# A 1024-step tanh recurrence on one core: split early sum, full tanh in PSUM, sums seeded by copies, rolled loops

## The chip, the cores and the metric

The kernel runs on one core of one Trainium2 chip. The metric is the device time of one execution in microseconds (us), lower is better. The kernel before was timed in three runs.

## The reference

The input `x` is 2 sequences of 1024 steps with 256 channels. Two residual layers follow each other. The first is a per-sequence 256x256 matrix (a base matrix plus a low-rank part made from a conditioning vector); the second is a recurrence over the 1024 steps:

```python
x = x + _L0_cond_ref(x, cond, ...)      # x + x @ layer, so y = 2 x + x @ layer
xW = einsum('ntd,dh->nth', y, Wx) + b
def step(prev_h, xw):
    next_h = tanh(prev_h @ Wh + xw)     # h0 = cond
x = y + h_t                             # every step's state is added to the output
```

Each step depends on the one before, and a step's work is tiny: two vectors of 256 channels. Channels lie on partitions, so a state is a tile of 128 partitions by 4 columns: 2 channel halves `m` times 2 sequences `b` (`COLS` = 4).

## The kernel before, in words

**Exact products from f16.** Weights are split into a high and a low f16 part (`wh_s[:, 0]`, `wh_s[:, 1]`), scaled by 256. The state of step u is used in three f16 forms: `h_pre`, an early estimate; `h_rnd`, the rounded full state; `h_lo`, the difference between the full f32 state `h_f` and `h_pre`.

**One step of the chain** (`chain_step`, L312 on PE; L467 to L476 on ACT; L560 on DVE). PE keeps two sums for the next state. The early sum lies in the PSUM bank `pre` and needs only `h_rnd` times the high weights (4 matmuls); ACT turns it into `h_pre` of the next step. The full sum lies in the bank `acc` and needs `h_pre` times high and low weights (8 matmuls) and `h_lo` times the high weights (4 matmuls); ACT turns it into `h_f` (L462) and `h_rnd` (L464). DVE makes `h_lo` from `h_f` and `h_pre` (L563). The order of PE's 16 matmuls is written out by hand, with a wait ahead of each new operand:

```python
pe.wait_ge(s_hpre[half], u + 1)      # 7 matmuls with h_pre follow
pe.wait_ge(s_hrnd[half], u + 1)      # 4 with h_rnd, the last signals s_presum; 1 with h_pre
pe.wait_ge(s_hlo[half], u + 1)       # 4 with h_lo, the last signals s_sum
```

**Side work.** The 1024 steps are 32 blocks of 32, each of two halves A and B of 16 steps. Between the steps PE also does the block's other matmuls: `layer_products` (L275, 32 a block, first layer of the next block), `input_products` (L283, the products with `Wx` and the bias). The latter are done three times a half, into `pre` and into the two banks `acc` for even and odd steps: 54 matmuls a half. `turn_x` and `turn_out` (L265, L270) are f32 transposes; `turn_out` in step 1 of a half is followed by three semaphore clears (`clear_states`, L306). DVE does the splits, the sum with y (`sum_out`) and the copy of the output rows (`row_out`) between its `h_lo`.

**Code.** PE, ACT and DVE run fully unrolled code: 21105 matmuls, each with a weight load. Only SyncE, which issues the loads of `x_in` and the stores of `o_row`, has a loop over blocks (L230).

## Time and profile before

| | before |
|---|---|
| median of 3 runs | 792.67 us (791.72 to 792.92) |
| the profiled execution | 791.64 us |
| its span, first to last instruction | 789.8 us |
| matmuls, and busy share of PE | 21105, 93% |
| busy share of ACT and DVE | 50%, 33% |
| granted clock of TensorE | 1.00 throughout |

The busy share of PE is a union of overlapping matmuls: one lasts about 165 ns in the records, though PE starts the next one long before. To see how fast PE could go one has to look at the distance between starts, not at the busy share.

### The profile page before, as it was taken

The page shows a single profiled execution, that of the slowest core. Times are in us where ns is not written, and L with a number is a line of the kernel's source. Part 1 is how long each engine was busy: PE and PEld are TensorE (multiplying, and loading weights), DVE is VectorE, ACT ScalarE, POOL GpSimd, SP SyncE. Part 2 cuts the span into 40 slices and gives each one's busy share as a digit, 9 for nine tenths or more (in the row PEclk, how much of TensorE's full clock was granted, in tenths as well). Part 3 has the DMA queues.
Part 4 walks back from the last instruction along what each step waited for, and adds up shares of the span by engine and source line. Part 5 has one row for each costly group of instructions (what it writes and reads, how often), then busy time and mean ns, then how long its engine had stood idle before and what let it go on. Part 6 is the DMA issues. An engine that isn't in the chain of part 4 may idle for free.

```text
span 789.8 us, 48134 instructions
## 1 busy us (share of the span) xinstructions
PE 736.8 (93%) x21105; PEld 679.7 (86%) x21105; DVE 258.3 (33%) x1411; ACT 396.4 (50%) x3092; POOL 6.4 (1%) x18
## 2 busy tenths in 40 slices
PE   6699999999999999999999999999999999999996
PEld 5688888888888888888888888888888888888885
DVE  6433333333333333332333332323333333333322
ACT  6355545555555555555555554555555555554554
POOL 3000000000000000000000000000000000000000
DMA  7000000000000000000000000000000000000000
GB/s 271 7 10 9 11 11 9 7 11 9 10 11 9 7 11 9 10 10 10 7 10 10 10 10 10 10 8 10 10 10 10 10 7 9 11 10 9 8 7 6
DMA packets 12285, 12.51 MB, mean 16 GB/s; under 512 B 1813, under 2 KB 11056, under 8 KB 12080
## 3 DMA queue, kind: packets, MB, share of 16 engines
q1 hardware_dynamic: 11984, 9.45, 4.1%
q8 instruction: 166, 2.72, 1.4%
q14 instruction: 39, 0.32, 0.1%
q0 software_dynamic: 96, 0.02, 0.0%
HBM read 7.36 MB, written 2.10 MB: 12 GB/s over the span
## 4 chain that ended last, share of the span: by engine, by line
PE 88%; ACT 6%; issue 3%; DMA 1%; SPq 1%; DVE 1%; DVEq 0%; another core or an unknown queue 0%
PE acc L320 48%; PE pre L320 16%; PE p_y L278 8%; PE acc L297 7%; ACT h_pre L456 6%; PE pre L297 4%; PE p_xo L273 2%; PE p_xo L268 1%; DMA x_in<-x_dram 1%; PE acc L294 1%; PE pre L294 1%; SPq L212 1%; PE p_y L413 0%; SPq L209 0%; DVE lay_s L684 0%
## 5 line engine op out<-in xcount | busy, mean ns | idle before, releaser
L320 PE MATMUL acc<-h_pre,wh_s 128*128 128x2 f16 x8192 | 504.8, 168 | 35.7
L320 PEld LDWEIGHTS acc<-h_pre,wh_s 128*128 128x128 f16 x8192 | 378.5, 106 | 90.6 <-ACT h_pre L456 73.5
L456 ACT ACTIVATE h_pre<-pre 128x4 f16<-128x4 f32 x1023 | 178.0, 174 | 377.8 <-PE pre L320 377.8
L563 DVE TENSOR_TENSOR h_lo<-h_f,h_pre 128x4 f16<-128x4 f32 x1024 | 166.8, 163 | 512.6 <-ACT h_f L462 511.5
L320 PE MATMUL pre<-h_rnd,wh_s 128*128 128x2 f16 x4092 | 263.4, 168 | 0.0
L320 PE MATMUL acc<-h_lo,wh_s 128*128 128x2 f16 x4096 | 250.9, 165 | 0.0
L320 PEld LDWEIGHTS pre<-h_rnd,wh_s 128*128 128x128 f16 x4092 | 190.6, 108 | 0.0
L320 PEld LDWEIGHTS acc<-h_lo,wh_s 128*128 128x128 f16 x4096 | 188.4, 104 | 0.0
L462 ACT ACTIVATE h_f<-acc 128x4 f32<-128x4 f32 x1024 | 177.9, 174 | 0.6 <-PE acc L320 0.6
L464 ACT ACTIVATE h_rnd<-acc 128x4 f16<-128x4 f32 x1022 | 173.2, 169 | 0.0
L297 PE MATMUL acc<-y_s,wx_s 128*128 128x16 f16 x2048 | 101.8, 175 | 0.0
L278 PE MATMUL p_y<-x_s,lay_s 128*128 128x32 f16 x1024 | 89.8, 236 | 2.2 <-DVE lay_s L684 2.2
L297 PEld LDWEIGHTS acc<-y_s,wx_s 128*128 128x128 f16 x2048 | 79.3, 104 | 0.1
L278 PEld LDWEIGHTS p_y<-x_s,lay_s 128*128 128x128 f16 x1024 | 59.9, 120 | 2.7 <-DVE lay_s L684 2.7
L297 PE MATMUL pre<-y_s,wx_s 128*128 128x32 f16 x1024 | 58.1, 188 | 0.0
L297 PEld LDWEIGHTS pre<-y_s,wx_s 128*128 128x128 f16 x1024 | 42.1, 104 | 0.0
L294 PE MATMUL acc<-ones,b_w 128*128 128x16 f16 x256 | 25.8, 174 | 1.4 <-DVE y_s L543 1.4
L273 PE MATMUL p_xo<-ident,o_sum 128*64 128x128 f32 x64 | 25.7, 402 | 0.6 <-DVE o_sum L552 0.6
L558 DVE COPY o_row<-p_xo 64x128 f32<-64x128 f32 x64 | 18.1, 283 | 4.6 <-remote 1.6
L294 PEld LDWEIGHTS acc<-ones,b_w 128*128 128x128 f16 x256 | 16.8, 104 | 1.5 <-issue 1.5
L268 PE MATMUL p_xo<-ident,x_in 128*128 128x128 f32 x32 | 14.6, 455 | 0.7 <-DMA x_in<-x_dram 0.7
L552 DVE TENSOR_TENSOR o_sum<-y_cur,h_f 128x64 f32<-128x64 f32 x64 | 14.0, 219 | 0.6 <-ACT h_f L462 0.6
(77 smaller groups left out, 161.1 us busy)
## 6 DMA issues: line engine op xcount, KB each, us to landing
w_f<-w_dram SPq DMA_DIRECT2D x8, 512.0 KB, 7.6
x_in<-x_dram SPq DMA_DIRECT2D x32, 64.0 KB, 2.3
out_dram<-o_row SPq DMA_DIRECT2D x64, 32.0 KB, 1.9
w_f<-w_dram SPq DMA_DIRECT2D x1, 256.0 KB, 2.7
base_f<-base_dram SPq DMA_DIRECT2D x1, 256.0 KB, 10.2
wh_f<-wh_dram SPq DMA_DIRECT2D x1, 256.0 KB, 9.8
wx_f<-wx_dram SPq DMA_DIRECT2D x1, 256.0 KB, 9.9
cond_r<-cond_dram SPq DMA_DIRECT2D x1, 2.0 KB
```

Of the source, the lines that this page charges most:

```text
L268: nc.tensor.transpose(p_xo[:, 0:P], x_in[:, :], ident[:, :]).then_inc(s_xturn, 1)
L273: nc.tensor.transpose(p_xo[0:HALF * COLS, 0:P], o_sum[:, :], ident[:, :]).then_inc(s_oturn, 1)
L278: last = nc.tensor.matmul(py[:, :, mo, bb], lay_s[:, pw, bb, ki, mo * P:(mo + 1) * P], x_s[:, px, :, ki, bb], start=(bb, mo, ki, pw, px) = ...
L294: nc.tensor.matmul(dst, b_w[:, out_channels], ones[:, 0:n * NB], start=mo == 0, stop=True, skip_group_check=True)
L297: nc.tensor.matmul(dst, wx_s[:, pw, ki, out_channels], y_s[:, py, t, ki, :], start=False, stop=True, skip_group_check=True)
L320: return nc.tensor.matmul(dst[:, mo, :], wh_s[:, pw, ki, mo * P:(mo + 1) * P], h[:, par, ki, :], start=False, stop=True, skip_group_check= ...
L456: nc.scalar.activation(h_pre[:, n % 2].rearrange("p m b -> p (m b)"), src, func, scale=scale).then_inc(s_hpre[(n // HALF) % 2], 1)
L462: nc.scalar.activation(h_f[:, (n - 1) % BLOCK, :], src, func, scale=scale).then_inc(s_hf[half], 1)
L464: nc.scalar.activation(h_rnd[:, n % 2].rearrange("p m b -> p (m b)"), src, func, scale=scale).then_inc(s_hrnd[half], 1)
L552: nc.vector.tensor_add(o_sum[:, :], cols(y_cur[:, steps]), h_f[:, steps, :].rearrange("p t c -> p (t c)")).then_inc(s_osum, 1)
L558: nc.vector.tensor_copy(o_row[:, :], p_xo[0:HALF * COLS, 0:P]).then_inc(s_orow, 1)
L563: nc.vector.tensor_sub(h_lo[:, par].rearrange("p m b -> p (m b)"), h_f[:, slot, :], h_pre[:, par].rearrange("p m b -> p (m b)")).then_inc( ...
```

## The change

- **Two-piece early part.** `pre` becomes two banks, one for each channel half `m`. PE signals `s_presum` after each 2 of the 4 `h_rnd` matmuls, and ACT makes `h_pre` in two activations of 2 columns, each with its own signal. PE waits for them one by one: 4 matmuls with channel half 0 of `h_pre`, 4 with half 1. All 8 now stand ahead of the `h_rnd` matmuls (7 before).
- **f32 tanh to PSUM.** The full state that DVE needs is written to a PSUM bank `p_f`; DVE subtracts from there. A third activation of the full sum writes `h_f` in SBUF for the output (`s_hkeep`).
- **Seeded sums.** `input_products` writes only `pre` (18 matmuls a half). DVE copies the even and odd steps from there into the two `acc` banks, now shared by both halves (`seed`); PE takes `s_seed` ahead of steps 10 and 11 of a half.
- **Side work moved.** Input products in steps 2 to 4 of a half, all 32 layer products in steps 8 to 12 of half A, `turn_x` in step 5, the semaphore clears in steps 6 and 7. `x_s` and the layer's sum are laid out with the step innermost.
- **Loops.** PE, ACT and DVE run the 30 middle blocks in a hardware loop each (`Fori`), whose body is one block of 32 steps.

```diff
-        acc = [[pb(f"acc{half}{par}", [P, 512]) for par in range(2)] for half in range(2)]
-        pre = [pb(f"pre{half}", [P, 512]) for half in range(2)]
-        p_xo = pb("p_xo", [P, 512])
-        p_y = pb("p_y", [P, 512])
+        acc = [pb(f"acc{par}", [P, 512]) for par in range(2)]
+        pre = [pb(f"pre{half}", [P, NM, 512]) for half in range(2)]
+        p_w = pb("p_w", [P, 512])
+        p_f = pb("p_f", [P, 512])
...
-        PRE = 2
-        INPUT = [(slot, *product) for slot in (0, PRE, 1) for product in PRODUCTS]
-        BEFORE = 2 * len(PRODUCTS)
+        INPUT = sorted(PRODUCTS, key=lambda product: product[0])
...
+        FILL, LAYERS, SEED = 2, 8, 10
+        def z_cols(half, u):
+            at = (half * (HALF // 2) + u // 2) * COLS
+            return slice(at, at + COLS)
...
             def input_products(half, todo):
...
+                t = slice(half * HALF, (half + 1) * HALF)
+                for mo, ki, pw, py in todo:
+                    dst = pre[half][:, mo, 0:HALF * NB]
...
             def chain_step(half, u, last=False):
                 par = u % 2
-                full = acc[half][par][:, (u // 2) * COLS:(u // 2 + 1) * COLS].rearrange("p (m b) -> p m b", b=NB)
-                early = pre[half][:, u * COLS:(u + 1) * COLS].rearrange("p (m b) -> p m b", b=NB)
+                full = acc[par][:, z_cols(half, u)].rearrange("p (m b) -> p m b", b=NB)
                 def onto(dst, pw, mo, ki, h):
-                    return nc.tensor.matmul(dst[:, mo, :], wh_s[:, pw, ki, mo * P:(mo + 1) * P], h[:, par, ki, :],
+                    return nc.tensor.matmul(dst, wh_s[:, pw, ki, mo * P:(mo + 1) * P], h[:, par, ki, :],
                                             start=False, stop=True, skip_group_check=True)
-                pe.wait_ge(s_hpre[half], u + 1)
-                for mo, ki in TILES:
-                    onto(full, 1, mo, ki, h_pre)
-                for mo, ki in TILES[:3]:
-                    onto(full, 0, mo, ki, h_pre)
+                for ki in range(NM):
+                    pe.wait_ge(s_hpre[half], NM * u + ki + 1)
+                    for mo in range(NM):
+                        for pw in range(2):
+                            onto(full[:, mo, :], pw, mo, ki, h_pre)
                 if not last:
                     pe.wait_ge(s_hrnd[half], u + 1)
-                    for mo, ki in TILES:
-                        done = onto(early, 0, mo, ki, h_rnd)
-                    done.then_inc(s_presum[half], 1)
-                for mo, ki in TILES[3:]:
-                    onto(full, 0, mo, ki, h_pre)
+                    for mo in range(NM):
+                        for ki in range(NM):
+                            done = onto(pre[half][:, mo, u * NB:(u + 1) * NB], 0, mo, ki, h_rnd)
+                        done.then_inc(s_presum[half], 1)
                 pe.wait_ge(s_hlo[half], u + 1)
                 for mo, ki in TILES:
-                    done = onto(full, 0, mo, ki, h_lo)
+                    done = onto(full[:, mo, :], 0, mo, ki, h_lo)
                 done.then_inc(s_sum[half], 1)
-            def half_a(first=False, last=False):
+            def half_steps(half, first=False, last=False):
                 for u in range(HALF):
-                    chain_step(A, u)
-                    if first and u == 0:
-                        input_products(A, INPUT[BEFORE:])
-                    if not first and u == 1:
+                    if u >= SEED and u < SEED + 2 and not (last and half == B):
+                        take(pe, s_seed[u % 2], 1)
+                    chain_step(half, u, last=last and half == B and u == HALF - 1)
+                    if u == 1 and not first:
                         turn_out()
-                        clear_states(B)
-                    if 2 <= u < 10:
-                        input_products(B, share(INPUT, 7, u - 2))
-                    if last:
-                        continue
-                    if u == 10:
-                        turn_x()
-                    if u == 13:
-                        take(pe, s_xsplit, 1)
-                    if 13 <= u < HALF - 1:
-                        layer_products(share(EARLY, 4, u - 13))
-            def half_b(last=False):
-                for u in range(HALF):
-                    chain_step(B, u, last=last and u == HALF - 1)
-                    if u == 1:
-                        turn_out()
-                        clear_states(A)
-                    if last:
-                        continue
-                    if u == 0:
-                        layer_products(share(LATE, 5, 0))
-                    if 2 <= u < 6:
-                        product = layer_products(share(LATE, 5, u - 1))
-                    if u == 5:
-                        product.then_inc(s_ymm, 1)
-                    if u == 9:
-                        take(pe, s_ysplit, 1)
-                    if 9 <= u < HALF - 1:
-                        input_products(A, share(INPUT, 9, u - 9))
+                    if FILL <= u < FILL + 3 and not (last and half == B):
+                        if u == FILL and half == B:
+                            take(pe, s_ysplit, 1)
+                        filled = input_products(1 - half, share(INPUT, 6, u - FILL))
+                        if u == FILL + 2:
+                            filled.then_inc(s_fill, 1)
+                    if u == 6 and not first:
+                        clear_states(1 - half)
+                    if u == 7 and not first:
+                        pe.sem_clear(s_hlo[1 - half])
+                    if half == A and not last:
+                        if u == 5:
+                            turn_x()
+                        if u == LAYERS:
+                            take(pe, s_xsplit, 1)
+                        if LAYERS <= u < LAYERS + 5:
+                            product = layer_products(share(LAYER, 7, u - LAYERS))
+                        if u == LAYERS + 4:
+                            product.then_inc(s_ymm, 1)
...
-            input_products(A, INPUT[:BEFORE])
-            half_a(first=True)
-            for _ in range(NBLOCK - 2):
-                half_b()
-                half_a()
-            half_b()
-            half_a(last=True)
-            half_b(last=True)
+            input_products(A, INPUT).then_inc(s_fill, 1)
+            for par in range(2):
+                take(pe, s_seed[par], 1)
+            half_steps(A, first=True)
+            with pe.Fori(0, NBLOCK - 2):
+                half_steps(B)
+                half_steps(A)
+            half_steps(B)
+            half_steps(A, last=True)
+            half_steps(B, last=True)
             turn_out()
...
         def _(act):
-            def give_pre(n, src, func, scale):
-                nc.scalar.activation(h_pre[:, n % 2].rearrange("p m b -> p (m b)"), src, func,
-                                     scale=scale).then_inc(s_hpre[(n // HALF) % 2], 1)
-            def give_h(n, src, func, scale, rounded=True):
+            def give_pre(n, m, src, func, scale):
+                nc.scalar.activation(h_pre[:, n % 2, m, :], src, func, scale=scale).then_inc(s_hpre[(n // HALF) % 2], 1)
+            def give_h(n, src, func, scale, rounded=True, final=False):
                 half = (n // HALF) % 2
-                nc.scalar.activation(h_f[:, (n - 1) % BLOCK, :], src, func, scale=scale).then_inc(s_hf[half], 1)
+                if not final:
+                    nc.scalar.activation(p_f[:, 0:COLS], src, func, scale=scale).then_inc(s_hf[half], 1)
                 if rounded:
                     nc.scalar.activation(h_rnd[:, n % 2].rearrange("p m b -> p (m b)"), src, func,
                                          scale=scale).then_inc(s_hrnd[half], 1)
+                nc.scalar.activation(h_f[:, (n - 1) % BLOCK, :], src, func, scale=scale).then_inc(s_hkeep[half], 1)
             def half_block(half, first=False, last=False):
                 for u in range(HALF):
                     final = last and u == HALF - 1
                     n = half * HALF + u + 1
                     if not final:
-                        act.wait_ge(s_presum[half], u + 1)
-                        give_pre(n, pre[half][:, u * COLS:(u + 1) * COLS], ACT.Tanh, 1.0 / SCALE)
+                        for m in range(NM):
+                            act.wait_ge(s_presum[half], NM * u + m + 1)
+                            give_pre(n, m, pre[half][:, m, u * NB:(u + 1) * NB], ACT.Tanh, 1.0 / SCALE)
                     act.wait_ge(s_sum[half], u + 1)
-                    give_h(n, acc[half][u % 2][:, (u // 2) * COLS:(u // 2 + 1) * COLS], ACT.Tanh, 1.0 / SCALE,
-                           rounded=not (last and u >= HALF - 2))
+                    give_h(n, acc[u % 2][:, z_cols(half, u)], ACT.Tanh, 1.0 / SCALE,
+                           rounded=not (last and u >= HALF - 2), final=final)
...
             half_block(A, first=True)
-            for _ in range(NBLOCK - 2):
+            with act.Fori(0, NBLOCK - 2):
                 half_block(B)
...
+            def seed(half, par):
+                early = pre[half][:, :, 0:HALF * NB].rearrange("p m (t q b) -> p t q m b", q=2, b=NB)[:, :, par]
+                at = half * (HALF // 2) * COLS
+                full = acc[par][:, at:at + (HALF // 2) * COLS].rearrange("p (t m b) -> p t m b", m=NM, b=NB)
+                nc.vector.tensor_copy(full, early).then_inc(s_seed[par], 1)
             def chain_step(half, u):
-                par, slot = u % 2, (half * HALF + u - 1) % BLOCK
+                par = u % 2
                 dve.wait_ge(s_hf[half], u + 1)
-                nc.vector.tensor_sub(h_lo[:, par].rearrange("p m b -> p (m b)"), h_f[:, slot, :],
+                nc.vector.tensor_sub(h_lo[:, par].rearrange("p m b -> p (m b)"), p_f[:, 0:COLS],
                                      h_pre[:, par].rearrange("p m b -> p (m b)")).then_inc(s_hlo[half], 1)
...
+                    if SEED - 1 <= u < SEED + 1 and not (last and half == B):
+                        if u == SEED - 1:
+                            take(dve, s_fill, 1)
+                        dve.wait_ge(s_hkeep[half], u + 1)
+                        seed(1 - half, (u - 1) % 2)
...
+            take(dve, s_fill, 1)
+            for par in range(2):
+                seed(A, par)
...
+            half_steps(A, first=True)
+            with dve.Fori(0, NBLOCK - 2):
```

**Where the instructions stand.** PE, one step of half A, before. `acc` is the full sum, `pre` the early sum, `wh_s` the recurrent weights:

```order
L320 MATMUL acc<-h_pre,wh_s 128x2 [waits s_hpreA]
L320 MATMUL acc<-h_pre,wh_s 128x2 x6
L320 MATMUL pre<-h_rnd,wh_s 128x2 [waits s_hrndA]
L320 MATMUL pre<-h_rnd,wh_s 128x2 x3
L320 MATMUL acc<-h_pre,wh_s 128x2
L320 MATMUL acc<-h_lo,wh_s 128x2 [waits s_hloA]
L320 MATMUL acc<-h_lo,wh_s 128x2 x3
```

and the same step after the change:

```order
L321 MATMUL acc<-h_pre,wh_s 128x2 [waits s_hpreA]
L321 MATMUL acc<-h_pre,wh_s 128x2 x3
L321 MATMUL acc<-h_pre,wh_s 128x2 [waits s_hpreA]
L321 MATMUL acc<-h_pre,wh_s 128x2 x3
L321 MATMUL pre<-h_rnd,wh_s 128x2 [waits s_hrndA]
L321 MATMUL pre<-h_rnd,wh_s 128x2 x3
L321 MATMUL acc<-h_lo,wh_s 128x2 [waits s_hloA]
L321 MATMUL acc<-h_lo,wh_s 128x2 x3
```

The lone `h_pre` matmul between the `h_rnd` and the `h_lo` group has moved to the front, and there is one more wait.

PE at the end of the loop's body (the last steps of half A; the branch goes back to the first step of half B, 583 matmuls earlier):

```order
L321 MATMUL acc<-h_lo,wh_s 128x2 [waits s_hloA]
L321 MATMUL acc<-h_lo,wh_s 128x2 x3
L435 REGISTER_ALU
L435 COMPARE_AND_BRANCH
L321 MATMUL acc<-h_pre,wh_s 128x2 [waits s_hpreB]
L321 MATMUL acc<-h_pre,wh_s 128x2 x3
```

Before, the program simply ran on there.

## Rows read from the trace of the kernel before

**Rows 1.** The page: span, PE's busy time, the chain that ended last by engine.

```profile
span 789.8 us, 48134 instructions
...
PE 736.8 (93%) x21105; PEld 679.7 (86%) x21105; DVE 258.3 (33%) x1411; ACT 396.4 (50%) x3092; POOL 6.4 (1%) x18
...
PE 88%; ACT 6%; issue 3%; DMA 1%; SPq 1%; DVE 1%; DVEq 0%; another core or an unknown queue 0%
```

**Rows 2.** Waits: engine line waited for: us in total, times, longest us.

```profile
PEld acc L320 <- ACT h_pre L456: 73.5, 332, 0.3
```

**Rows 3.** Timeline of ACT, h_pre of three steps: start us, us, what, idle before.

```profile
387.32 0.17 ACT L456 ACTIVATE h_pre<-pre 128x4 f16<-128x4 f32 x1 [0.36 <-PE pre L320]
...
397.59 0.17 ACT L456 ACTIVATE h_pre<-pre 128x4 f16<-128x4 f32 x1 [0.36 <-PE pre L320]
...
398.39 0.17 ACT L456 ACTIVATE h_pre<-pre 128x4 f16<-128x4 f32 x1 [0.43 <-PE pre L320]
```

**Rows 4.** Timeline of one step without side work (PEld is the weight load).

```profile
401.32 0.17 ACT L456 ACTIVATE h_pre<-pre 128x4 f16<-128x4 f32 x1 [0.36 <-PE pre L320]
401.45 0.17 ACT L462 ACTIVATE h_f<-acc 128x4 f32<-128x4 f32 x1
401.53 0.17 ACT L464 ACTIVATE h_rnd<-acc 128x4 f16<-128x4 f32 x1
401.55 0.27 PEld L320 LDWEIGHTS acc<-h_pre,wh_s 128*128 128x128 f16 x7 [0.21 <-ACT h_pre L456]
...
401.66 0.16 DVE L563 TENSOR_TENSOR h_lo<-h_f,h_pre 128x4 f16<-128x4 f32 x1 [0.31 <-ACT h_f L462]
...
401.75 0.19 PEld L320 LDWEIGHTS pre<-h_rnd,wh_s 128*128 128x128 f16 x4
...
401.88 0.18 PEld L320 LDWEIGHTS acc<-h_lo,wh_s 128*128 128x128 f16 x4
...
402.06 0.17 ACT L456 ACTIVATE h_pre<-pre 128x4 f16<-128x4 f32 x1 [0.36 <-PE pre L320]
402.19 0.17 ACT L462 ACTIVATE h_f<-acc 128x4 f32<-128x4 f32 x1
```

**Rows 5.** Timeline around turn_out and the clears that follow it on PE.

```profile
385.72 0.13 PEld L273 LDWEIGHTS p_xo<-ident,o_sum 128*64 128x64 f32 x1
...
385.78 0.17 ACT L456 ACTIVATE h_pre<-pre 128x4 f16<-128x4 f32 x1 [0.36 <-PE pre L320]
...
386.09 0.27 PEld L320 LDWEIGHTS acc<-h_pre,wh_s 128*128 128x128 f16 x7 [0.24 <-ACT h_pre L456]
```

**Rows 6.** Timeline of the start: weight loads in a row, and the chain's first h_pre.

```profile
25.79 1.73 PEld L278 LDWEIGHTS p_y<-x_s,lay_s 128*128 128x128 f16 x32 [2.70 <-DVE lay_s L684]
...
29.10 0.51 PEld L297 LDWEIGHTS acc<-y_s,wx_s 128*128 128x128 f16 x16
...
30.50 0.17 ACT L456 ACTIVATE h_pre<-pre 128x4 f16<-128x4 f32 x1 [4.60 <-PE pre L320]
```

**Rows 7.** Timeline of the start: DVE reading PSUM after PE; ACT reading SBUF.

```profile
17.92 2.07 PE L413 MATMUL p_y<-hid_s,w_s 128*128 128x4 f16 x32
...
20.10 0.23 DVE L657 TENSOR_TENSOR ab_sum<-p_y,b_c 128x64 f32<-128x64 f32 x1 [0.53 <-PE p_y L413]
...
25.51 0.20 ACT L456 ACTIVATE h_pre<-cond_c 128x4 f16<-128x4 f32 x1
```

**Rows 8.** DMA queues of the page: packets, MB, share of 16 engines.

```profile
q8 instruction: 166, 2.72, 1.4%
q14 instruction: 39, 0.32, 0.1%
```

**Rows 9.** DMA issues of the page: count, KB each, median us from issue to landing.

```profile
x_in<-x_dram SPq DMA_DIRECT2D x32, 64.0 KB, 2.3
out_dram<-o_row SPq DMA_DIRECT2D x64, 32.0 KB, 1.9
```

**Rows 10.** Costliest groups of the page: the input products into the full sum.

```profile
L297 PE MATMUL acc<-y_s,wx_s 128*128 128x16 f16 x2048 | 101.8, 175 | 0.0
```

More of the change, by code:

```diff
@@ L44 @@
 NBLOCK = T // BLOCK
-PAIRS = HALF // 2
 SCALE = 256.0
@@ L102, in cond_recurrence @@
         x_f = sb("x_f", [P, BLOCK, NM, NB])
-        x_s = sb("x_s", [P, 2, BLOCK, NM, NB], F16)
+        x_s = sb("x_s", [P, 2, NM, NB, BLOCK], F16)
         y_new = sb("y_new", [P, BLOCK, NM, NB])
@@ L157, in cond_recurrence @@
         s_hlo = [sem("s_hloA"), sem("s_hloB")]
+        s_hkeep = [sem("s_hkeepA"), sem("s_hkeepB")]
+        s_fill = sem("s_fill")
+        s_seed = [sem("s_seed0"), sem("s_seed1")]
         s_xload = sem("s_xload")
@@ L181, in cond_recurrence @@
         cols = lambda ap: ap.rearrange("p t m b -> p (t m b)")
+        by_step = lambda ap: ap.rearrange("p m b t -> p t m b")
         def take(eng, s, n):
@@ L398, in _ @@
                 for k in range(NM):
-                    last = nc.tensor.matmul(p_xo[:, 256 + mo * NB:256 + (mo + 1) * NB], w1_f[:, k, mo * P:(mo + 1) * P],
+                    last = nc.tensor.matmul(p_w[:, 256 + mo * NB:256 + (mo + 1) * NB], w1_f[:, k, mo * P:(mo + 1) * P],
                                             ae[:, k, :], start=k == 0, stop=k == NM - 1)
@@ L412, in _ @@
                         w = w2_s[:, pw, k, tile_of_ab(q)].rearrange("p (d r) -> p r d", r=RANK)
-                        last = nc.tensor.matmul(p_y[:, c:c + 2 * NB], w[:, r, :],
+                        last = nc.tensor.matmul(pre[B][:, 0, c:c + 2 * NB], w[:, r, :],
                                                 hid_s[:, k].rearrange("p s b -> p (s b)"),
@@ L418, in _ @@
             for q in range(4):
-                last = nc.tensor.matmul(pre[A][0:NB * 4 * RANK, q * P:(q + 1) * P],
+                last = nc.tensor.matmul(pre[A][0:NB * 4 * RANK, 0, q * P:(q + 1) * P],
                                         ab_st[:, q].rearrange("p b s r -> p (b s r)"), ident16[:, :],
@@ L427, in _ @@
                 for k in range(NM):
-                    last = nc.tensor.matmul(acc[A][bb][:, k * D:(k + 1) * D], ab_t[rows, k, :],
+                    last = nc.tensor.matmul(acc[bb][:, k * D:(k + 1) * D], ab_t[rows, k, :],
                                             ab_t[rows, 2:4, :].rearrange("p k d -> p (k d)"), start=k == 0, stop=True,
@@ L488, in _ @@
                 for dst in (hid_s[:, m, 0, :], hid[:, m, :]):
-                    last = nc.scalar.activation(dst, p_xo[:, 256 + m * NB:256 + (m + 1) * NB], ACT.Gelu, bias=vec_c[:, 2, m:m + 1])
+                    last = nc.scalar.activation(dst, p_w[:, 256 + m * NB:256 + (m + 1) * NB], ACT.Gelu, bias=vec_c[:, 2, m:m + 1])
             last.then_inc(s_hidhi, 1)
@@ L508, in _ @@
             act.wait_ge(s_condc, 1)
-            give_pre(0, cond_c[:, :], ACT.Copy, 1.0)
+            for m in range(NM):
+                give_pre(0, m, cond_c[:, m * NB:(m + 1) * NB], ACT.Copy, 1.0)
             give_h(0, cond_c[:, :], ACT.Copy, 1.0)
             half_block(A, first=True)
-            for _ in range(NBLOCK - 2):
+            with act.Fori(0, NBLOCK - 2):
                 half_block(B)
@@ L689, in _ @@
             split_y_low()
+            take(dve, s_fill, 1)
+            for par in range(2):
+                seed(A, par)
             keep_y()
-            half_a(first=True)
-            for _ in range(NBLOCK - 2):
-                half_b()
-                half_a()
-            half_b()
-            half_a(last=True)
-            half_b(last=True)
-            dve.wait_ge(s_hf[A], 1)
+            half_steps(A, first=True)
+            with dve.Fori(0, NBLOCK - 2):
+                half_steps(B)
+                half_steps(A)
+            half_steps(B)
+            half_steps(A, last=True)
+            half_steps(B, last=True)
+            dve.wait_ge(s_hkeep[A], 1)
             sum_out(B)
```

94 lines of the change are left out of this document (40 added, 54 removed).

## The prediction

> **What bounds the kernel now.** I read the page first: PE is busy 93% of the span and holds 88% of the chain that ended last [rows 1]. That looks like a PE at its limit, but the waits say otherwise: PE does idle for ACT's `h_pre` in 332 places [rows 2]. So I went to the timeline of ACT and measured the step itself. `h_pre` starts at 387.32 and, 14 steps later, at 397.59: 0.733 us a step [rows 3], and the steps in between carry very different amounts of side work. The step is a fixed latency; side work lies in its idle part.
>
> One bare step shows the latency's parts [rows 4], all measured from start to start. Weight loads in a row are 0.027 us apart: 16 of them take 0.51 with a last one of 0.10 [rows 6]. ACT's `h_pre` (401.32) to PE's first load with it (401.55): 0.23. The last of the 4 `h_rnd` loads is at 401.75 + 3 x 0.027 = 401.83, and ACT starts the next `h_pre` at 402.06: 0.23 from the load. `h_f` follows when the last `h_lo` matmul is in: load at 401.88 + 0.08 = 401.96, ACT at 402.19, again 0.23. `h_rnd` starts 0.07 behind `h_f`, and PE's load with it is 0.22 later (401.75). `h_f` at 401.45 lets DVE start at 401.66 (0.21), which takes 0.16; PE's load with `h_lo` stands at 401.88. Three chains run around this ring:
>
> - early: 0.23 + 10 distances (7 + 4 loads) x 0.027 + 0.23 = 0.73;
> - rounded: `h_f` to `h_rnd` 0.07-0.08, to PE 0.22, 8 distances (4 + 1 + 4 loads) 0.21, 0.23: 0.73;
> - low: 0.21 + 0.16, about 0.05 to PE (the 0.05 from ACT's end at 401.49 to PE's load at 401.55), 3 distances 0.08, 0.23: 0.73.
>
> All three meet at 0.73 us: shortening one gives nothing.
>
> The whole adds up: first `h_pre` of the chain at 30.50 [rows 6], 1023 steps x 0.7336 = 750.5, and 62 late steps. Those are the steps behind `turn_out`, 0.80 instead of 0.73 [rows 3]: three clears (and the one of the wait) sit around the transpose, and the next load comes 0.31 after `h_pre` instead of 0.23 [rows 5]. 62 x 0.07 = 4.3. That is 785.3, with some 4.5 us for the irregular first step, the last output and the edges.
>
> **The change, part by part.** The sum is made against the profiled execution, 791.64 us, which is 1.0 below the median of 792.67.
>
> *Fewer matmuls.* 72 input products a block go, about 2300 of 21105 [rows 1, 10]. They lie in PE's idle time: between the last `h_lo` load (401.96 in [rows 4]) and the next `h_pre` load (402.28) fit 0.32 / 0.027 = 11, and up to 9 stood there. Gain 0. The new shares of 6 and 7 fit too. The innermost-step layout of `x_s` speeds up the layer products, whose loads stood 1.73 / 32 = 0.054 apart [rows 6]; hidden for the same reason.
>
> *The clears.* One clear stays behind `turn_out`; two come in step 6 and one in step 7. By [rows 5] four clears in a row cost 0.08, so one or two cost nothing. Gain up to 4; the waits for `s_seed` cost some back. DVE's copy of 32 columns can start behind the third activation, about `h_f` + 0.35, takes some 0.2 (the 64-column `ab_sum` takes 0.23 [rows 7]), and reaches PE at `h_f` + 0.6; the load of step 10 is due at `h_f` + 0.77, and needs perhaps 0.1 after its clear. It is hidden by 0.07; without this cover it would cost that much in 4 steps a block, 9 us. I take -3 in all.
>
> *Order and split.* Early chain: 0.23, now 8 + 2 loads, thus 9 distances 0.24, and 0.23: 0.70. Rounded chain: the lone matmul between is gone, 7 distances instead of 8: 0.70 to 0.71. ACT has five activations a step: 5 x 0.07 = 0.35 of 0.7; `h_f` stands 6 loads behind the first `h_pre`, 0.16, and ACT is free by then (2 x 0.07). Not a bound.
>
> *Low chain.* This one has no matmul removed. It stays at 0.73 unless the way over PSUM is shorter. Nothing in this trace has ACT write PSUM. Lower bound: ACT takes 0.17 with a PSUM input and 0.20 with an SBUF one [rows 4, 7], so a PSUM access may save 0.03. Upper bound: DVE started 0.11 after PE's modelled end at 19.99 [rows 7], while it starts 0.04 after ACT's end on SBUF data (401.62 to 401.66 in [rows 4]), so a PSUM input may add 0.07. I take 0.01 less, since the writer and the reader should nearly cancel, and the step becomes 0.72: 1023 x 0.013 = 13 us gained. Bounds: 0.705 (29 us gained, the other two chains then rule) and 0.80 (68 lost).
>
> *Loops.* 30 iterations, 29 branches back on each of three engines. What a branch back costs is not in the trace; what code costs is. PE's code comes in 166 fetches of 16 KB, which is all of its 42210 loads and matmuls at 64 bytes, and each packet takes 0.014 x 16 x 789.8 / 166 = 1.07 us [rows 8]. In straight code the fetches run ahead, and no step is late for one. The body is 583 matmuls, 1166 instructions, 75 KB: four to five such fetches behind PE. If the code at its head is no longer there, PE fetches it while the ring stands still; ACT's body of 160 activations may do the same at the same time, side by side. Lower bound, code kept: 0 to 0.3 a branch; the nearest row is again the clears, sequencer work too, at 0.08 for four [rows 5], and I leave room for some three times that. Upper bound: latency of the smallest regular transfer 1.9 [rows 9] plus the packet 1.07, and one more step of 0.7 to get going: 3.7. Instructions already queued on PE hide a part, perhaps a step. I take 1.9, the row nearest to it: 29 x 1.9 = 55 us lost.
>
> The Trainium skill ("Runtime: NRT & Kernel Launch", Instruction fetch mechanics) says that prefetch is purely sequential, and that a taken branch whose target isn't in the current two-page window stalls for a fetch. The fetches of [rows 8] agree with code being streamed; no run here shows the stall yet.
>
> **Sum:** 791.6 - 13 - 3 + 55 = 831 us.
>
> **The rivals.**
>
> *1. The code of a whole body stays near the engine (chance 0.24).* Then a branch back costs 0.3 us or less and the ring hides part of it. For it: 75 KB is not much, and SyncE's small loop costs nothing visible. Against it: PE's code is fetched at the rate at which it is used, up to the end. Time: 791.6 - 13 - 3 + 0 to 9, 776 to 785; with the step at 0.705, 760 to 769. This is the case on the other side. It decides below a branch cost of 16 / 29 = 0.55 us. The same page of the skill gives PE a code memory of 128 KiB, 2048 instructions, which would hold this body if it were kept; that stands against its own two-page rule.
>
> *2. DVE pays for reading PSUM (0.12).* The low chain becomes 0.78 to 0.80. With the loops' cost this gives 791.6 - 3 + 48 to 68 + 55 = 892 to 912; with free loops 837 to 857. For it the 0.11 of [rows 7]; against it the ends of matmuls are modelled, so that 0.07 may be no more than this. The skill ("VectorE: DVE Perf Modes", The TRN2 errata) gives VectorE a fixed 120 cycles with a PSUM source and 58 with an SBUF source. By that page's cycles the estimate would be 65 ns more a step. The skill ("ScalarE: Activation LUTs") also says that ScalarE's way to PSUM is the shorter, without a number; no row here shows either.
>
> *3. The stall is the full fetch, or PE's clock falls with it (0.14).* 3.0 to 3.7 a branch: 791.6 - 16 + 87 to 107 = 863 to 883. The granted clock is 1.00 throughout now, with no idle time of that length; at half clock the distances of 0.027 would be 0.054, some 0.25 us more a step for a few steps.
>
> *4. The fetches fit the stall but not fully (my forecast, 0.50).* 1.2 to 2.8 a branch, 800 to 860.
>
> **How the numbers follow.** Below 791 lies rival 1 (0.24, less a little where PSUM eats its gain): faster 0.23. A measurement can tell about 0.2% (1.6 us) from no change; same is a narrow coincidence, 0.03. Slower 0.74. The predicted time is that of the likeliest case, 831. The range leaves out the best corner of rival 1 and the worst of 2 and 3: 768 to 882. Within the slower cases alone I would give 800 to 882.
>
> **What would show it.** In the changed kernel's timeline: 29 gaps one block apart (every 23 us), on PE, right behind step 15 of a half A and ahead of `h_pre` of half B, each about 2 us; the code fetches of PE should not fall to a few, but stay near one per 256 instructions, about 145. Between them the step of `h_pre` should read 0.72, and the steps behind `turn_out` no longer 0.80. The start from `h_f` to `h_lo` on DVE (0.21 now) shows the way over PSUM: above 0.25 rival 2 holds. I am wrong if the gaps are missing or below 0.5 us, or if the fetches of code nearly vanish (rival 1).

## The result, and the profile after

| | before | after |
|---|---|---|
| median | 792.79 us (791.72 to 793.28) | 778.62 us (777.50 to 779.52) |
| the profiled execution | 791.64 us | 779.52 us |
| its span | 789.8 us | 777.7 us |
| granted TensorE clock, mean | 1.00 | 1.00 |

The ratio is 0.982, with a 95% interval of 0.9805 to 0.9835. The changed kernel is faster by 1.8%. The forecast was 831 us, slower; what came is the case on the other side, rival 1, whose time was worked out as 776 to 785. The range of the forecast, 768 to 882, holds the time only because it was drawn wide enough to take in that rival.

The page of the changed kernel, the parts that answer to [rows 1, 8]:

```profile
span 777.7 us, 46140 instructions
...
PE 694.6 (89%) x18801; PEld 626.4 (81%) x18801; DVE 305.6 (39%) x1539; ACT 501.1 (64%) x5140; POOL 6.4 (1%) x18
...
q8 instruction: 15, 0.25, 0.1%
...
q14 instruction: 6, 0.05, 0.0%
...
PE 70%; ACT 19%; DVE 5%; issue 3%; DMA 1%; SPq 1%; DVEq 0%; another core or an unknown queue 0%
```

PE's code came in 166 fetches before and comes in 15 now, ACT's and DVE's in 39 and now 6. The loop's code is fetched once. Both signs that the prediction named for being wrong, no gaps of 2 us at the branches and hardly any fetches, are there.

The timeline around a branch back on PE (its record lies between the two groups of loads, at 90.55, 0.21 us long). Columns as in [rows 4]:

```profile
90.44 0.18 PEld L321 LDWEIGHTS acc<-h_lo,wh_s 128*128 128x128 f16 x4
...
90.58 0.23 ACT L447 ACTIVATE h_pre<-pre 128x2 f16<-128x2 f32 x2 [0.24 <-PE pre L321]
...
90.82 0.29 PEld L321 LDWEIGHTS acc<-h_pre,wh_s 128*128 128x128 f16 x8 [0.19 <-ACT h_pre L447]
```

PE's first load with the new `h_pre` comes 0.24 behind it, where the step below has 0.22, and the step is no longer than its neighbours (`h_pre` at 89.87, 90.58 and 91.30). The branch fits into the wait for `h_pre` and costs nothing.

One step of the ring, and `h_pre` 17 steps earlier:

```profile
388.18 0.23 ACT L447 ACTIVATE h_pre<-pre 128x2 f16<-128x2 f32 x2 [0.24 <-PE pre L321]
...
400.31 0.24 ACT L447 ACTIVATE h_pre<-pre 128x2 f16<-128x2 f32 x2 [0.24 <-PE pre L321]
...
400.48 0.16 ACT L453 ACTIVATE p_f<-acc 128x4 f32<-128x4 f32 x1
400.53 0.29 PEld L321 LDWEIGHTS acc<-h_pre,wh_s 128*128 128x128 f16 x8 [0.18 <-ACT h_pre L447]
...
400.55 0.17 ACT L455 ACTIVATE h_rnd<-acc 128x4 f16<-128x4 f32 x1
...
400.67 0.16 DVE L567 TENSOR_TENSOR h_lo<-p_f,h_pre 128x4 f16<-128x4 f32 x1 [0.55 <-ACT p_f L453]
...
400.77 0.19 PEld L321 LDWEIGHTS pre<-h_rnd,wh_s 128*128 128x128 f16 x4
...
400.88 0.18 PEld L321 LDWEIGHTS acc<-h_lo,wh_s 128*128 128x128 f16 x4
...
401.02 0.23 ACT L447 ACTIVATE h_pre<-pre 128x2 f16<-128x2 f32 x2 [0.24 <-PE pre L321]
401.19 0.16 ACT L453 ACTIVATE p_f<-acc 128x4 f32<-128x4 f32 x1
```

The step is (400.31 - 388.18) / 17 = 0.713 us, against 0.733 before [rows 3]. `h_rnd` stands 0.07 behind `p_f`, PE's load with it 0.22 later, the last load with `h_lo` 7 distances later (400.88 + 0.08 = 400.96), and `p_f` again 0.23 behind that (401.19): 0.71, the rounded chain as the prediction drew it. The low chain is as long at this resolution: `p_f` to `h_lo` 0.19, where `h_f` to `h_lo` took 0.21 [rows 4], then 0.21 to PE, 3 distances 0.08 and 0.23: 0.71. Which of the two rules is settled by one of the experiments below: it is the low chain, by some 0.007. No step behind `turn_out` is late any more.

One place in each block is late, in half A. These are the rows of it:

```profile
408.24 0.71 DVE L521 CAST x_s<-p_w 128x128 f16<-128x128 f32 x1
...
408.58 0.38 DVE L567 TENSOR_TENSOR h_lo<-p_f,h_pre 128x4 f16<-128x4 f32 x1
...
408.88 0.23 ACT L447 ACTIVATE h_pre<-pre 128x2 f16<-128x2 f32 x2 [0.24 <-PE pre L321]
408.99 0.72 DVE L525 TENSOR_TENSOR x_s<-p_w,x_s 128x128 f16<-128x128 f32 x1
...
409.03 0.18 PEld L321 LDWEIGHTS acc<-h_lo,wh_s 128*128 128x128 f16 x4 [0.22 <-DVE h_lo L567]
...
409.53 0.18 DVE L567 TENSOR_TENSOR h_lo<-p_f,h_pre 128x4 f16<-128x4 f32 x1
...
409.88 0.23 ACT L447 ACTIVATE h_pre<-pre 128x2 f16<-128x2 f32 x2 [0.24 <-PE pre L321]
```

The two splits of `x_s` take 0.71 and 0.72 (0.28 before) and cannot be passed by `h_lo`, which is next on DVE. `h_lo` is late, PE waits 0.22 for it, and one step becomes 409.88 - 408.88 = 1.00; with the two steps ahead of it and the one behind it the loss is 0.34 a block (407.44 to 410.64 for `h_pre`, 3.20 where four steps take 2.85). In the waits it is the 31 times that PE waited for `h_lo`:

```profile
PEld acc L321 <- ACT h_pre L447: 100.0, 554, 0.4
...
PEld acc L321 <- DVE h_lo L567: 7.1, 31, 0.6
```

**The ledger.** The chain's `h_pre` ran from 30.50 to 785.19 before, 754.7 us, and from 32.80 to 773.00 after, 740.2 us. Of the 14.5 between them, 1022 steps x 0.020 = 20.4 come from the step; 4.3 from the steps behind `turn_out`; 31 x 0.34 = 10.5 are given back around `x_s`: -14.2. The chain also starts 2.3 later, and what lies behind it is the same. -14.5 + 2.3 = -12.2, and the spans differ by 12.1. The start itself varies from profile to profile of like programs: the kernel before with loops (below) starts its chain at 32.07, the changed kernel without them at 31.09. So the 2.3, or a part of it, need not be an effect of the change.

### The profile page after: what moved, and what is told of

Its sections match the earlier page's. It is cut to its first block, busy times and chain, and to the rows that moved or that the text cites. A ratio compares the mean times of both kernels' runs of the same rounds, so it can differ in the third digit from the quotient of the medians.

```text
span 777.7 us, 46140 instructions
## 1 busy us (share of the span) xinstructions
PE 694.6 (89%) x18801; PEld 626.4 (81%) x18801; DVE 305.6 (39%) x1539; ACT 501.1 (64%) x5140; POOL 6.4 (1%) x18
## 4 chain that ended last, share of the span: by engine, by line
PE 70%; ACT 19%; DVE 5%; issue 3%; DMA 1%; SPq 1%; DVEq 0%; another core or an unknown queue 0%
PE acc L321 45%; ACT h_pre L447 17%; PE pre L321 14%; PE p_w L285 4%; PE pre L301 4%; DVE x_s L521 3%; PE p_w L280 2%; DMA w_f<-w_dram 1%; DVE x_f L520 1%; ACT p_f L453 1%; DVE h_lo L567 1%; PE pre L298 1%; SPq L219 1%; ACT h_rnd L455 0%; ACT w_s L493 0%
## 5 line engine op out<-in xcount | busy, mean ns | idle before, releaser
L321 PE MATMUL acc<-h_pre,wh_s 128*128 128x2 f16 x8192 | 384.8, 168 | 55.4 <-DVE acc L562 1.0
L447 ACT ACTIVATE h_pre<-pre 128x2 f16<-128x2 f32 x2046 | 240.7, 170 | 251.5 <-PE pre L321 251.5
L321 PEld LDWEIGHTS acc<-h_pre,wh_s 128*128 128x128 f16 x8192 | 302.0, 106 | 116.1 <-ACT h_pre L447 100.0
L567 DVE TENSOR_TENSOR h_lo<-p_f,h_pre 128x4 f16<-128x4 f32 x1024 | 173.1, 169 | 449.7 <-ACT p_f L453 449.5
L453 ACT ACTIVATE p_f<-acc 128x4 f32<-128x4 f32 x1023 | 161.6, 158 | 7.2 <-PE acc L321 7.2
L285 PE MATMUL p_w<-x_s,lay_s 128*128 128x32 f16 x1024 | 52.8, 188 | 2.2 <-DVE lay_s L684 2.2
L285 PEld LDWEIGHTS p_w<-x_s,lay_s 128*128 128x128 f16 x1024 | 39.5, 104 | 2.8 <-DVE lay_s L684 2.7
L280 PE MATMUL p_w<-ident,o_sum 128*64 128x128 f32 x64 | 26.1, 407 | 0.6 <-DVE o_sum L549 0.6
L562 DVE COPY acc<-pre 128x32 f32<-128x32 f32 x128 | 25.5, 200 | 1.4 <-PE pre L301 1.1
L298 PE MATMUL pre<-ones,b_w 128*128 128x32 f16 x128 | 24.2, 189 | 1.4 <-DVE y_s L540 1.4
## 6 DMA issues: line engine op xcount, KB each, us to landing
w_f<-w_dram SPq DMA_DIRECT2D x8, 512.0 KB, 10.2
```

Source lines behind the costliest of these rows:

```text
L280: nc.tensor.transpose(p_w[0:HALF * COLS, 0:P], o_sum[:, :], ident[:, :]).then_inc(s_oturn, 1)
L285: last = nc.tensor.matmul(py[:, mo, bb, :], lay_s[:, pw, bb, ki, mo * P:(mo + 1) * P], x_s[:, px, ki, bb, :], start=(bb, mo, ki, pw, px) = ...
L298: last = nc.tensor.matmul(dst, b_w[:, out_channels], ones[:, :], start=True, stop=True, skip_group_check=True)
L321: return nc.tensor.matmul(dst, wh_s[:, pw, ki, mo * P:(mo + 1) * P], h[:, par, ki, :], start=False, stop=True, skip_group_check=True)
L447: nc.scalar.activation(h_pre[:, n % 2, m, :], src, func, scale=scale).then_inc(s_hpre[(n // HALF) % 2], 1)
L453: nc.scalar.activation(p_f[:, 0:COLS], src, func, scale=scale).then_inc(s_hf[half], 1)
```

## The experiments

### The loops alone, both ways

The change with its three loops written out (`for _ in range(NBLOCK - 2)` on PE, ACT and DVE), and the kernel before with its bodies in loops:

```diff
-            for _ in range(NBLOCK - 2):
+            with pe.Fori(0, NBLOCK - 2):
```

> The changed kernel with its three loops written out again. The prediction's loop term (55 us lost) is void if this is within 2 us of 778.6: the branch back is then free. The theory that loops even help (less code traffic) would make this one 3 to 10 us slower. If a hidden cost of the branches exists, this is faster by 29 x that cost. About 150 more code fetches for PE are expected in the DMA rows.

Measured: 778.00 us (777.38 to 778.44), ratio 0.9817 (0.980 to 0.983), step 0.713. 148 fetches of code on PE's queue, 57 on that of ACT and DVE.

> The kernel before, with nothing but the three loops. A body has 655 matmuls, 1310 PE instructions. If a body of this size is kept near the engine: 792.8 us, equal to before within 0.3%, and some 20 code fetches for PE instead of 166. By the prediction's own term it would be 55 us slower, 848.

Measured: 792.90 us (792.37 to 793.63), ratio 1.0006 (0.9997 to 1.0015), step 0.733. 16 and 5 fetches.

So the loops cost nothing and bring nothing in either kernel beyond 1 us, though PE's body has 1166 loads and matmuls in one and 1310 in the other (1183 and 1323 instructions with the clears and the branch). The whole gain is in the rest of the change.

### Where a loop starts to cost

PE's loop with two blocks in its body, 2332 loads and matmuls (2364 instructions in all) and 14 branches back:

```diff
-            with pe.Fori(0, NBLOCK - 2):
-                half_steps(B)
-                half_steps(A)
+            with pe.Fori(0, (NBLOCK - 2) // 2):
+                for _ in range(2):
+                    half_steps(B)
+                    half_steps(A)
```

> The changed kernel with PE's loop body doubled to two blocks: 1166 matmuls, 2332 instructions, 149 KB, 14 branches back instead of 29. ACT and DVE keep their bodies. Theory K (PE keeps 2048 instructions, eight fetches of 256): the target of the branch is no longer there, each branch back stalls for a fetch and the fetches return, about 9 to 10 per iteration, 140 in all; by the sizes of the prediction 1.2 to 3.7 us a branch, so 17 to 52 us slower, 796 to 830. Rival (the memory is larger or the branch is foreseen): 778.6 and still 15 fetches.

Measured: 827.18 us (826.00 to 828.24), ratio 1.0433 (1.042 to 1.045); 173 fetches on PE's code queue. The timeline at the first branch back of this kernel, and its waits for nothing that the profile shows:

```profile
91.28 0.23 ACT L448 ACTIVATE h_pre<-pre 128x2 f16<-128x2 f32 x2 [0.24 <-PE pre L321]
...
94.94 0.29 PEld L321 LDWEIGHTS acc<-h_pre,wh_s 128*128 128x128 f16 x8 [3.62 <-issue]
...
95.41 0.23 ACT L448 ACTIVATE h_pre<-pre 128x2 f16<-128x2 f32 x2 [3.66 <-PE pre L321]
```

```profile
PEld acc L321 <- issue: 50.7, 15, 3.8
```

The time from `h_pre` to `h_pre` is 4.13 in place of 0.71: a branch back costs 3.4 us, and 14 of them are the 48 us that this kernel is over the changed one (the 15th wait is a short one at the start). The records of the taken branches themselves last 3.3 to 3.8 us, against 0.21 in the changed kernel. This is the stall that the prediction feared, real and dearer than the 1.9 taken, but it does not occur in a body of 1166. TensorE's clock does not fall with it: granted 1.00 from 91.3 to 94.9, in the stall, and the 8 loads behind it take 0.29 as elsewhere. That settles the clock in the prediction's rival 3.

The same kernel with the assembler's hint at the loop's head that the branch at its end will be taken:

```diff
-            with pe.Fori(0, (NBLOCK - 2) // 2):
+            with nc.Fori(0, (NBLOCK - 2) // 2, engines=[mybir.EngineType.PE], hint_back_edge=True):
```

> PE's loop body of two blocks (827.2 us without it) with one instruction at the head of each iteration that tells PE's sequencer in advance where the closing branch goes. If the 3.2 us at each of the 14 branches is the fetch of the code at the head of the loop, this lets the fetch run ahead: branch records of 0.2 to 0.3 us instead of 3.6, and 778 to 783 us. If the stall is something else that a large body brings, it stays at 827.

Measured: 786.48 us (785.56 to 788.08), ratio 0.9927 (0.991 to 0.994), still 160 fetches. Of the 48 us 8 are left, some 0.56 a branch; the branch's records last 0.54 to 0.83 us. That is more than the 0.2 to 0.3 and the 778 to 783 us expected. The code is still fetched at each turn. The drop from 3.4 to 0.56 fits a fetch that starts ahead of the branch; no row shows the fetch itself.

To bracket the size, idle matmuls were put into step 13 of half A (250 and 350 of them, each with its load; their sum goes to columns of `pre` that nothing reads), and ACT's loop got two and three blocks. Both start from the dense version below.

```diff
+                        if u == LAYERS + 5 and not first:
+                            for _ in range(250):
+                                nc.tensor.matmul(pre[B][:, 0, 64:64 + NB], wh_s[:, 0, 0, 0:P], ones[:, 0:NB],
+                                                 start=False, stop=True, skip_group_check=True)
```

> The dense-write version with 250 idle matmuls (onto unused columns of the other half's early bank) behind step 13 of half A in the loop, so that PE's body is about 1680 instructions, and ACT's body doubled to about 336. Only the branch records and code fetches are read here; the time itself is longer by 30 x 250 x 0.027 = 200 us for the idle matmuls, about 965. If PE keeps up to 2048 instructions: its branches stay at 0.2 us. If ACT keeps 512: its branches stay at 0.045 us; if it keeps 256, they rise to some 3 us.

One run: 958.67 us; the idle matmuls are what it has over the dense version. With the clears and the branch PE's body is 1683 instructions, ACT's 330. 17 and 7 fetches; PE's branch record 0.21 us, ACT's 0.05: both bodies are kept.

One run: 1135.34 us. PE's body is 1883 instructions, ACT's 494. Its page and its waits:

```profile
q8 instruction: 278, 4.55, 1.6%
...
q14 instruction: 63, 0.52, 0.1%
```

```profile
PEld acc L321 <- issue: 99.7, 30, 3.7
```

Every one of 29 turns stalls PE for 3.3 to 3.7 us again (the 30th wait is the short one at the start). PE keeps a body of 1683 and not one of 1883. ACT's code is fetched anew as well (63), but whether that alone would stall ACT stays open: its branch lies within PE's stall.

### The write of `x_s`

DVE writes `x_s` in the order in which it lies, and takes `p_w` in strides instead:

```diff
-            px = p_w[:, 0:P].rearrange("p (t m b) -> p t m b", m=NM, b=NB)
+            px_m = p_w[:, 0:P].rearrange("p (t m b) -> p m b t", m=NM, b=NB)
...
-                nc.vector.tensor_copy(by_step(x_s[:, 0]), px).then_inc(s_own, 1)
+                nc.vector.tensor_copy(x_s[:, 0], px_m).then_inc(s_own, 1)
...
-                nc.vector.tensor_sub(by_step(x_s[:, 1]), px, by_step(x_s[:, 0])).then_inc(s_xsplit, 1)
+                nc.vector.tensor_sub(x_s[:, 1], px_m, x_s[:, 0]).then_inc(s_xsplit, 1)
```

> The changed kernel with one edit: DVE makes the two f16 parts of x with the step innermost, so that it writes x_s densely and reads the PSUM bank with a stride. Theory S (a scattered f16 write is what makes these two operations 0.71 us long, and 0.34 us of that comes through to the step chain in each of 31 blocks): both fall to 0.28 to 0.30 us, the three late steps of a block vanish, and the time falls by 31 x 0.34 = 10.5 us and some 0.8 us more in the start, to about 767 us. Rival (any strided operand of this size is slow): they stay at about 0.7 us and the time stays at 778.6.

Measured: **767.89 us** (767.54 to 768.87), ratio 0.9694 (0.968 to 0.971), the fastest of all kernels here. The groups of the changed kernel, and then of this one:

```profile
L525 DVE TENSOR_TENSOR x_s<-p_w,x_s 128x128 f16<-128x128 f32 x32 | 22.9, 717 | 1.0
L521 DVE CAST x_s<-p_w 128x128 f16<-128x128 f32 x32 | 22.7, 709 | 0.0
```

```profile
L525 DVE TENSOR_TENSOR x_s<-p_w,x_s 128x128 f16<-128x128 f32 x32 | 9.0, 281 | 0.0
L521 DVE CAST x_s<-p_w 128x128 f16<-128x128 f32 x32 | 9.0, 281 | 0.0
```

The chain runs from 31.04 to 761.03, 730.0 us: 10.2 less than after the change. So of the 10.5 in the ledger 10.2 are the write of `x_s`; the rest is the step with `turn_x`, which stays. The scattered write costs 2.5 times the time; the strided read of f32 from PSUM costs nothing over the dense one (281 ns, as for the dense cast before).

Is the layout then of any use? The old one again, with the step outermost in `x_s` and in the layer's sum, and all else as in the changed kernel (only PE's side is shown; DVE's two splits and its sum with `p_w` go by the same order):

```diff
-        x_s = sb("x_s", [P, 2, NM, NB, BLOCK], F16)
+        x_s = sb("x_s", [P, 2, BLOCK, NM, NB], F16)
-                    ... nc.tensor.matmul(py[:, mo, bb, :], ..., x_s[:, px, ki, bb, :], ...)
+                    ... nc.tensor.matmul(py[:, :, mo, bb], ..., x_s[:, px, :, ki, bb], ...)
```

> The changed kernel with the old layout of x_s and of the layer's sum (step outermost): DVE reads and writes densely, PE reads x_s and writes its sum with a stride. Theory S (only the scattered f16 write is dear, and PE's strided layer products lie in idle time): DVE's two operations at 0.28, layer products' loads 0.045 to 0.054 apart instead of 0.027, 7 of them 0.35 us, just about hidden: 768, like the dense-write version, at most 31 x 5 x 0.1 = 15 us more if they push the next step. Rival (the layout of x_s has nothing to do with it): 778.

Measured: 779.55 us (779.09 to 780.06), ratio 0.9836 (0.982 to 0.985), the same as the changed kernel within a microsecond. By the time alone this would be the rival, that the layout has nothing to do with it; the rows say otherwise. DVE's splits are back at 280 ns, but now the layer products are late. Groups of this kernel, and then `h_pre` in three of its layer steps:

```profile
L285 PE MATMUL p_w<-x_s,lay_s 128*128 128x32 f16 x1024 | 80.0, 238 | 2.2 <-DVE lay_s L684 2.2
...
L285 PEld LDWEIGHTS p_w<-x_s,lay_s 128*128 128x128 f16 x1024 | 58.4, 123 | 2.7 <-DVE lay_s L684 2.7
```

```profile
408.77 0.23 ACT L447 ACTIVATE h_pre<-pre 128x2 f16<-128x2 f32 x2 [0.24 <-PE pre L321]
409.58 0.24 ACT L447 ACTIVATE h_pre<-pre 128x2 f16<-128x2 f32 x2 [0.34 <-PE pre L321]
410.38 0.24 ACT L447 ACTIVATE h_pre<-pre 128x2 f16<-128x2 f32 x2 [0.33 <-PE pre L321]
```

Four steps a block take 0.80 instead of 0.71: 31 x 4 x 0.09 = 11 us. Seven layer products a step need the innermost-step layout to fit; what it gives to PE, the scattered write takes on DVE, and the dense write has both.

### Each part of the change taken back

The early part in one piece again (PE waits once for `h_pre`, ACT makes it in one activation), order and `p_f` kept:

```diff
+                pe.wait_ge(s_hpre[half], u + 1)
                 for ki in range(NM):
-                    pe.wait_ge(s_hpre[half], NM * u + ki + 1)
```

> The changed kernel with the early part in one piece again: PE signals once behind all 4 h_rnd matmuls, ACT makes h_pre in one activation of 4 columns over both banks, PE waits once. Order of matmuls, full tanh in PSUM and seeding stay. Theory of the three chains: the early chain now has 8 + 4 loads, 11 distances of 0.027, so 0.22 + 0.29 + 0.23 = 0.74 us a step instead of 0.713; 1023 x 0.027 = 28 us more, 806. Rival (the split only spreads ACT's work and another chain rules): 0.713 and 778.6.

Measured: 808.25 us (807.90 to 808.38), ratio 1.0201 (1.018 to 1.022), step 0.747.

The full tanh straight to `h_f` in SBUF, where DVE reads it, without `p_f` and the third activation:

```diff
-                nc.vector.tensor_sub(h_lo[...], p_f[:, 0:COLS], h_pre[...])
+                nc.vector.tensor_sub(h_lo[...], h_f[:, slot, :], h_pre[...])
```

> The changed kernel with the full tanh written to h_f in SBUF only, as before: no p_f, no third activation, DVE subtracts from SBUF. The split, the order and the seeding stay. Theory P (the way over PSUM is what took the low chain below 0.73): the step goes back to 0.73, 1023 x 0.018 = 18 us more, 797. Rival N (the low chain was never the limit, the earlier 0.73 came from the other two): 0.713 and 778.6, or slightly less, since ACT has one activation less.

Measured: 794.52 us (794.16 to 796.75), ratio 1.0029 (1.002 to 1.004), step 0.733. Two rows of its timeline against the ring above: DVE starts 0.21 behind the activation instead of 0.19, and PE's load with `h_lo` comes 0.22 behind DVE instead of 0.21.

```profile
400.69 0.17 ACT L452 ACTIVATE h_f<-acc 128x4 f32<-128x4 f32 x1
...
400.90 0.16 DVE L565 TENSOR_TENSOR h_lo<-h_f,h_pre 128x4 f16<-128x4 f32 x1 [0.44 <-ACT h_f L452]
...
401.12 0.19 PEld L321 LDWEIGHTS acc<-h_lo,wh_s 128*128 128x128 f16 x4
```

Both at once, so that only the order of the matmuls is new in the ring:

> The changed kernel with both taken back: early part in one piece and full tanh in SBUF. What is left of the change in a step is the order of the matmuls (8, 4, 4 instead of 7, 4, 1, 4). By the chains the early one rules with 11 distances: 0.74 a step, slower than the kernel before by 0.007 x 1023, some 7 us, less the 5 us of the clears, plus 10 for the scattered x_s: about 806. If the rounded chain ruled alone, this would be 0.706 a step and about 775.

Measured: 807.70 us (807.19 to 808.28), ratio 1.0194 (1.018 to 1.021), step 0.747.

One of the 8 matmuls with `h_pre` back between `h_rnd` and `h_lo`, in two pieces and with `p_f`:

```diff
+                            if (pw, mo, ki) != (1, 1, 1):
+                                onto(full[:, mo, :], pw, mo, ki, h_pre)
...
+                onto(full[:, 1, :], 1, 1, 1, h_pre)
```

> The changed kernel with one of the 8 h_pre matmuls moved back between the h_rnd and the h_lo group (7, 4, 1, 4). The rounded chain gets its 8th distance back. If it rules: 0.713 + 0.027 = 0.740 a step, 27 us more, 806. If the early chain rules: 0.686 to 0.713, no slower than 778.6.

Measured: 796.68 us (795.23 to 797.91), ratio 1.0054 (1.004 to 1.007), step 0.733: longer by 0.020, where 0.740 and 806 us had been expected, a whole distance of 0.027 more. One step of its timeline:

```profile
411.76 0.16 ACT L455 ACTIVATE p_f<-acc 128x4 f32<-128x4 f32 x1
...
411.83 0.17 ACT L457 ACTIVATE h_rnd<-acc 128x4 f16<-128x4 f32 x1
...
411.95 0.16 DVE L569 TENSOR_TENSOR h_lo<-p_f,h_pre 128x4 f16<-128x4 f32 x1 [0.57 <-ACT p_f L455]
412.05 0.18 PEld L321 LDWEIGHTS pre<-h_rnd,wh_s 128*128 128x128 f16 x4
...
412.19 0.18 PEld L321 LDWEIGHTS acc<-h_lo,wh_s 128*128 128x128 f16 x4
...
412.49 0.16 ACT L455 ACTIVATE p_f<-acc 128x4 f32<-128x4 f32 x1
```

Here PE takes `h_lo` 0.24 behind DVE's start, later than the 0.21 that it needs, so the low chain has room and the rounded chain rules at 0.733. With one distance less the rounded chain alone would be 0.706. The changed kernel's 0.713 lies above that: in it the low chain rules, and the rounded one has some 0.007 to spare; hence the miss of this run. The starts agree: in the median of its bare steps PE's first load with `h_lo` stands 0.033 behind the last with `h_rnd`, where loads in a row stand 0.027 apart.

The four together say what the ring is. With any one part missing the step is 0.733 or more, and the order alone makes it longer than before, because the eighth matmul with `h_pre` then stands ahead of the last one with `h_rnd` in a chain that still has one piece: 0.23 + 11 distances x 0.027 + 0.23 = 0.757 on paper, where the two 0.23 are rounded up, and 0.747 measured. Only all three together give 0.713. The seeds and the moved side work were not taken back one by one; what they do is read from the trace only.

## Why the prediction was wrong

**The step that failed: "if the code at its head is no longer there".** The term for the loops (+55, bounds 0 to 0.3 and 3.7 a branch) stood on two questions: does PE still have the code, and what does it pay if not. The first was answered wrongly. A body of 1166 loads and matmuls is kept, so is one of 1683 instructions in all, and a branch back within them costs nothing: its 0.21 us lie in PE's wait for `h_pre`. The argument against rival 1, that PE's code is fetched at the rate of its use up to the end, says nothing on this: straight code is never used twice, and no fetch in the trace of before could have told whether old code is kept. That was no evidence, and a chance of 0.24 on the case was too low for a question that the trace could not speak to. The Trainium skill ("Runtime: NRT & Kernel Launch", Instruction fetch mechanics) says that a taken branch out of the current two-page window stalls. By that rule the loops would have cost 29 stalls; the runs show none at 1183, 1323 and 1683 instructions, and stalls at 1883 and 2364. The same page's code memory of 128 KiB is the nearer description, though the edge lies somewhat below its 2048 instructions.

**The price of a stall** was the second question. The upper bound, 1.9 + 1.07 + 0.7 = 3.7, was nearly right: 3.4 are measured where the code is gone (4.13 less 0.71), within rival 3's 3.0 to 3.7 and well over the 1.9 taken. The guess that instructions queued on PE hide perhaps a step of it was wrong: the branch records last 3.6 us on average and 3.4 of that reaches the ring, which needs the very next instructions. What the 3.4 are made of, latency and packet as the prediction had it or something else, stays open.

**Clears and `turn_out`**, taken at -3: the late steps behind `turn_out` are all gone, -4.3, and the two steps that wait for the seeds take 0.713 like the others.

**Order and split**: the rounded chain came out at 0.706, within the 0.70 to 0.71 drawn; the early one was put at 0.70 and never seen to rule. **Low chain**: the way over PSUM was taken as 0.01 shorter, with 0.03 shorter and 0.07 longer as bounds. It is 0.02 shorter (0.733 without it, 0.713 with it). The low chain still rules, as forecast: step 0.713 instead of 0.72, -20.4 instead of -13. The mechanism was right, the size nearer the better bound. Most of it is in the writer: ACT's own operation takes 158 ns to PSUM and 174 to SBUF, and DVE starts about 0.03 behind its end in both. Rival 2 is out: DVE starts no later on PSUM data than on SBUF data (0.19 against 0.21). The Trainium skill ("VectorE: DVE Perf Modes", The TRN2 errata) gives a PSUM source more fixed cycles than an SBUF one. The estimate of 65 ns more that its cycles make does not show here: `h_lo` takes 163 ns from SBUF before and 162 from PSUM in the version with the dense write. (The 169 in the changed kernel is a mean with the 31 slow ones beside `x_s`.)

```profile
L563 DVE TENSOR_TENSOR h_lo<-h_f,h_pre 128x4 f16<-128x4 f32 x1024 | 166.8, 163 | 512.6 <-ACT h_f L462 511.5
```

```profile
L567 DVE TENSOR_TENSOR h_lo<-p_f,h_pre 128x4 f16<-128x4 f32 x1024 | 165.9, 162 | 460.1 <-ACT p_f L453 459.9
```

**A term that was not there:** the layout of `x_s` was costed at nothing on the side of PE, and its writer was not priced at all. DVE's scattered writes gave back 10.2 us, about half of what the ring won. The sentence "hidden for the same reason" was wrong on the side of PE too: without the layout four steps a block are late, 11 us.

By its own steps with the measured terms the sum reads 791.6 - 20.4 - 4.3 + 10.5 + 0 + 2.3 for the later start = 779.7, with 779.5 measured. That the time fell into rival 1's 776 to 785 is in part luck: the ring and the clears gave 8.7 us more than the 16 taken, and the write of `x_s` and the later start, neither of them in the sum, took 12.8. The rest of the forecast (PE bound by a fixed latency, fewer matmuls worth nothing) fits: about 2300 matmuls went and PE's busy share fell from 93% to 89%, but before the change none of the steps that held them was late, so there was nothing to gain there.

## What to carry to other kernels

A loop needs no fear as long as its body on each engine stays well inside what the engine keeps (here 1683 of PE's instructions, 330 of ACT's); ask for the body's size before the price of a miss. In a ring of chains that tie, price the whole set of edits, not each: here no two of the three brought the step below 0.733, and the order alone made it longer. And when a layout is changed for its reader, price its writer on the engine where it stands in a queue with the ring's own work.

## What the runs showed that I had not expected

- PE keeps a loop body of 1683 instructions and not one of 1883; beyond it each turn costs 3.4 us, and the hint at the loop's head lowers that to 0.56.
- DVE's f16 write to SBUF with 64 bytes from most elements to the next takes 709 to 717 ns for 128 elements, 281 dense: 3.4 ns more for each element. A strided f32 read from PSUM in its place costs nothing (281).
- ACT writes 4 columns of f32 to PSUM in 158 ns. To SBUF it takes 174 in the same place (the kernel before, and the one with `h_f` in SBUF only) and 182 as the third activation of the changed kernel:

```profile
L457 ACT ACTIVATE h_f<-acc 128x4 f32<-128x4 f32 x1024 | 186.4, 182 | 0.5 <-PE acc L321 0.5
...
L453 ACT ACTIVATE p_f<-acc 128x4 f32<-128x4 f32 x1023 | 161.6, 158 | 7.2 <-PE acc L321 7.2
```
